# Inverse softmax sums moved from the probabilities to the weighted values in three attention layers

## The reference, cut to what matters

```python
# layer 0: 16 heads of 32; layer 1: 16 query heads of 32, 4 key heads, sparse mask; layer 2: 8 heads of 64, 1 key head
scores = jnp.einsum('bhqd,bhkd->bhqk', qn, kn) + attn_bias
p = jax.nn.softmax(scores, axis=-1)
o = jnp.einsum('bhqk,bhkd->bhqd', p, v)
o = jnp.transpose(o, (0, 2, 1, 3)).reshape(Bs, Lx, Cx)
x = x + (o @ Wproj.T + bproj) * gamma1        # layer 0 alone has gamma and a projection bias
```

## Time and profile before

| | |
|---|---|
| median of 3 runs | 2899.52 us (2898.2 to 2907.24) |
| profiled execution | 2904.38 us, span from first to last instruction 2902.6 us |
| mean granted TensorE clock | 0.894 |
| PE busy | 2427.1 us, 84% of the span |
| DVE busy | 1624.0 us, 56% |
| ACT busy | 1213.8 us, 42% |
| POOL busy | 908.3 us, 31% |

### The profile page before, as it was taken

The page is one execution under the profiler, slowest core; times in us unless marked ns, Lnnn a source line. Parts: engine busy times, 40 slices in busy tenths (PEclk is TensorE's granted clock), DMA queues, the critical chain, the costliest instruction groups (busy, mean ns, idle before and its releaser), DMA issues. The chain is left out here.

```text
span 2902.6 us, 47820 instructions
## 1 busy us (share of the span) xinstructions
PE 2427.1 (84%) x15668; PEld 1962.4 (68%) x15668; DVE 1624.0 (56%) x4635; ACT 1213.8 (42%) x2990; POOL 908.3 (31%) x982
## 2 busy tenths in 40 slices
PE   4878789798589999688888568889689999996786
PEld 2767677677477888466666457777578888885565
DVE  3777766677654443566556466566543333333876
ACT  2565565566331111366656445556431111112443
POOL 0234332233376676223223113223212112110422
PEclk7989889899899999788678679999899999997898
DMA  6000000000200000100000000000101000001000
GB/s 230 1 1 1 9 2 9 1 2 9 88 15 30 15 29 0 71 30 2 2 1 1 31 4 1 1 0 1 46 20 37 30 22 22 0 0 47 1 29 29
DMA packets 15887, 63.16 MB, mean 22 GB/s; under 512 B 2604, under 2 KB 3500, under 8 KB 10692
## 3 DMA queue, kind: packets, MB, share of 16 engines
q1 hardware_dynamic: 15684, 60.65, 5.8%
HBM read 56.42 MB, written 4.23 MB: 21 GB/s over the span
## 5 line engine op out<-in xcount | busy, mean ns | idle before, releaser
L871 ACT ACTIVATE l0a_prob<-l0a_prob,l0a_nmin 128x512 f32<-128x512 f32 x256 | 185.8, 726 | 202.9 <-DVE l0a_nmin L1129 202.5
L1673 POOL TENSOR_TENSOR l2m_hidl<-l2m_hid,l2m_hidh 128x512 fp32r<-128x512 f32 x64 | 100.9, 1577 | 480.2 <-DVE l2m_hidh L1645 480.2
L1293 POOL TENSOR_TENSOR l0a_prob<-l0a_prob,l0a_rinv 128x512 f32<-128x512 f32 x64 | 66.7, 1042 | 517.9 <-DVE l0a_rinv L1136 517.9
L1529 ACT ACTIVATE l2m_gate<-l2m_psG 128x512 f32<-128x512 f32 x64 | 38.3, 598 | 452.0 <-PE l2m_psU L1462 452.0
L1640 DVE TENSOR_TENSOR l2m_hid<-l2m_gate,l2m_psU 128x512 f32<-128x512 f32 x64 | 44.0, 688 | 300.1 <-ACT l2m_gate L1529 300.1
L702 PE MATMUL l0a_psT<-res_ident,l0a_prob 128*128 128x128 f32 x1024 | 166.2, 287 | 12.0 <-ACT l0a_PT L881 11.8
L1129 DVE CUSTOM_DVE_ANT_0 l0a_prob<-l0a_psS,l0a_mask 128x512 f32<-128x512 f32 x256 | 173.3, 688 | 2.6 <-issue 1.6
L1692 POOL TENSOR_TENSOR res_X<-res_X,l0m_share 128x512 f32<-128x512 f32 x128 | 161.8, 1292 | 25.7 <-DVE l0m_share L1629 24.7
L680 PE MATMUL l0a_psS<-l0a_kT,l0a_qT 96*128 96x512 f32 x256 | 127.9, 501 | 43.5 <-DVE l0a_nmin L1129 28.6
L560 PE MATMUL l0a_psA<-l0a_wh,l0a_hTh 128*128 128x128 f32 (+1 forms) x512 | 152.2, 297 | 12.7 <-DVE l0a_wl L1244 5.8
L702 PEld LDWEIGHTS l0a_psT<-res_ident,l0a_prob 128*128 128x128 f32 x1024 | 133.9, 148 | 38.9 <-ACT l0a_PT L881 17.9
(11 more groups left out here) (399 smaller groups left out, 7785.3 us busy)
## 6 DMA issues: line engine op xcount, KB each, us to landing
l2m_stage<-in_l2m_w SPq DMA_DIRECT2D x8, 1536.0 KB, 6.7
l0m_stage<-in_l0m_w SPq DMA_DIRECT2D x8, 1024.0 KB, 4.8
cond_w<-in_wmod SPq DMA_DIRECT2D x6, 1024.0 KB, 7.9
res_X<-in_x SPq DMA_DIRECT2D x4, 1024.0 KB, 13.4
l0a_prob<-in_l0a_w SPq DMA_DIRECT2D x4, 1024.0 KB, 6.6
l1a_wmod<-in_wmod SPq DMA_DIRECT2D x4, 1024.0 KB, 6.0
out<-res_X SPq DMA_DIRECT2D x4, 1024.0 KB, 4.3
l_stage<-in_l_w SPq DMA_DIRECT2D x3, 1024.0 KB, 7.2
```

Source lines behind the costliest of these rows:

```text
L871: act.activation(prob[:, n % NP, 0:w], src[:, 0:w], ACT.Exp, bias=nmin[:, n % NP:n % NP + 1], scale=-1.0, accum_out=ssum[:, n % NP:n % NP ...
L1293: op = pool.tensor_tensor(x, x, r.to_broadcast([P, w]), ALU.mult)
L1673: pool.tensor_tensor(hidl[:, s % 2, m, :], hid[:, m, :], f32(hidh[:, s % 2, m, :]), ALU.subtract).then_inc(hl_done, 1)
```

## The change

POOL no longer multiplies the probabilities; they are turned and weighed as exp gave them. Per unit it writes one tile `rwide`: the four inverse sums of each query, repeated over the 32 (L2: 64) features of each head, 128 x 128 (L2: 128 x 256). Twice in a group a new PE job "rT" turns two such tiles (step 9 of the group and step 2 of the next) into psA, and ACT copies them to SBUF tile rT, which then lies as psO does: features down, queries across. After the group's last `weigh`, DVE multiplies psO by rT into rT (`o_scale`, step 7). `o_copy` moves to step 8 and `o_rest` to step 9, and both read rT. The next group's `weigh` waits for `o_scale` alone. In L0 the tile bG is gone: G holds first the row to add, then gamma, with a second load between, and POOL adds to X at the end of a batch. L0's output jobs move from steps 9, 10, 11, 20 to 10, 11, 19, 21. The conditioning tiles shrink, padded copies of them are made where they are used (`padded_rows`), and the small table `pick` is loaded in three places.

```diff
+                    elif kind == "rT":
+                        pe.wait_ge(rw_done, 4 * g + 2 * x + 2)
+                        for o in range(NO):
+                            for t in range(2):
+                                c0 = (2 * o + t) * P
+                                mm = pe.transpose(psA[i][:, c0:c0 + P], rwide[:, t, o, :], R.ident[:])
+                        mm.then_inc(rT_mm, 1)
+                        freed[i] = [(rT_done, 2 * g + (x + 1))]
...
-                    pe.wait_ge(p_done, b * NTILE + (m + 1))
+                    pe.wait_ge(exp_done, b * NTILE + (m + 1))
...
-                        pe.wait_ge(oh_done, b * NG * NO + u // NT * NO)
-                        pe.wait_ge(ol_done, b * NG * NO + u // NT * NO)
+                        pe.wait_ge(on_done, b * NG * NO + u // NT * NO)
...
+                    elif kind == "rT":
+                        act.wait_ge(rT_mm, 2 * g + (x + 1))
+                        if x == 0:
+                            act.wait_ge(ol_done, NO * g)
+                        act.activation(rT[:, :, x * 2 * P:(x + 1) * 2 * P],
+                                       psA[i][:, 0:NO * 2 * P].rearrange("p (o q) -> p o q", o=NO),
+                                       ACT.Copy).then_inc(rT_done, 1)
...
+                def o_scale(b, hg):
+                    v.wait_ge(pv_done, b * U + (hg + 1) * NT)
+                    v.wait_ge(rT_done, 2 * (b * NG + hg + 1))
+                    for o in range(NO):
+                        v.tensor_tensor(rT[:, o, :], psO[o][:], rT[:, o, :], ALU.mult).then_inc(on_done, 1)
...
-                        act.activation(oTh[:, k, :], psO[o][:], ACT.Identity, bias=bias).then_inc(oh_done, 1)
+                        act.activation(oTh[:, k, :], rT[:, o, :], ACT.Identity, bias=bias).then_inc(oh_done, 1)
...
-                        for j in range(4):
-                            s = (4 * u + j) % NP
-                            x, r = prob[:, s, 0:w], rinv[:, s:s + 1]
-                            if j == 0:
-                                op = pool.tensor_tensor(x, x, r.to_broadcast([P, w]), ALU.mult)
-                            else:
-                                op = pool.tensor_scalar(x, x, r, 1.0, ALU.mult, ALU.mult)
-                            op.then_inc(p_done, 1)
...
+                def widen(b, u, first):
+
+                    pool.wait_ge(rinv_done, b * U + u + 1)
+                    if u % 2 == 0 and not (first and u == 0):
+                        pool.wait_ge(rT_mm, b * 2 * NG + u // 2)
+                    r = rinv[:, u % 2].rearrange("p (o j) -> p o j", o=NO)[:, :, :, None].to_broadcast(
+                        [P, NO, 4 // NO, HD])
+                    pool.tensor_tensor(rwide[:, u % 2].rearrange("p o (j d) -> p o j d", d=HD), r,
+                                       R.zero[:, :, None, None].to_broadcast([P, NO, 4 // NO, HD]),
+                                       ALU.add).then_inc(rw_done, 1)
...
-        OUT_AT = (9, 10, 11, 20) if is0 else (12, 13, 14, 15)
+        OUT_AT = (10, 11, 19, 21) if is0 else (12, 13, 14, 15)
+        RT_AT = {9: (0, 0), 2: (-1, 1)}
...
-                        sp.dma_start(G[:], bcast_rows(D["gam_rows"][0, b])).then_inc(g_in, 16)
-                        sp.dma_start(bG[:], bcast_rows(D["gam_rows"][1, b])).then_inc(g_in, 16)
+                        sp.dma_start(G[:], bcast_rows(D["gam_rows"][1, b])).then_inc(g_in, 16)
+                        sp.wait_ge(xg_done, b + 1)
+                        sp.dma_start(G[:], bcast_rows(D["gam_rows"][0, b])).then_inc(g_in, 16)
```

More of the change, by code:

```diff
@@ L114, in modulation_products, with modulation_sums, padded_rows @@
     return mm
-def modulation_sums(pe, R, rows, ps):
+def modulation_sums(pe, pick, rows, ps):
     for m in range(NK):
-        mm = pe.matmul(ps[:, m * B:(m + 1) * B], rows[:, m * P:(m + 1) * P], R.pick[:], start=True, stop=True)
+        mm = pe.matmul(ps[:, m * B:(m + 1) * B], rows[:, m * P:(m + 1) * P], pick[:], start=True, stop=True)
     return mm
+def padded_rows(pool, R, c32, c32_zero, c32_done):
+    pool.memset(c32[:], 0.0).then_inc(c32_zero, 1)
+    pool.wait_ge(c32_zero, 1)
+    pool.tensor_copy(c32[:, 0, :, 0:B], R.sc[:])
+    pool.tensor_copy(c32[:, 1, :, 0:B], R.cT[:]).then_inc(c32_done, 1)
 def modulation_bias(v, R, g, ps):
@@ L149, in condition @@
         rows = S.sb("rows", [P, 2, C])
+        pick = S.sb("pick", [P, B])
+        c32 = S.sb("c32", [P, 1, NK, COLS])
+        c32_zero = S.sem("c32_zero")
         pm = [S.ps(f"pm{i}", [P, 512]) for i in range(2)]
@@ L205, in sums @@
                         pe.wait_ge(mod_read, g - 1)
-                    modulation_sums(pe, R, rows[:, g % 2], ps[g % 2]).then_inc(mod_sum, 1)
+                    modulation_sums(pe, pick, rows[:, g % 2], ps[g % 2]).then_inc(mod_sum, 1)
                 pe.wait_ge(silu_done, 1)
@@ L441, in jobs @@
             todo = []
+            if s in RT_AT and n <= NTILE + 2 and not (first and n == 2):
+                todo.append(("rT", hg + RT_AT[s][0], RT_AT[s][1]))
             if hg < NG:
@@ L486, in banked @@
         def banked(first, more, last):
-            n_, out = 0, []
+            n_, out = int(first), []
             for n in range(NTILE + (OUT_AT[-1] + 2 if last else 0)):
@@ L900, in batch @@
                             pT_copy(b, m - CL, first)
[L901 removed]
+                        if n % GS == LAG + 2 and n <= NTILE + LAG + 2 and not (first and n == LAG + 2):
                             o_copy(b, n // GS - 1)
@@ L1150, in o_rest @@
                         bias = R.vb[:, k:k + 1] if is0 else R.zero[:]
-                        v.scalar_tensor_tensor(oTl[:, k, :], psO[o][:], bias, f32(oTh[:, k, :]), ALU.add,
+                        v.scalar_tensor_tensor(oTl[:, k, :], rT[:, o, :], bias, f32(oTh[:, k, :]), ALU.add,
                                                ALU.subtract).then_inc(ol_done, 1)
@@ L1219, in batch @@
                                 norm_rows(b + 1, NORM_T.index(s - NORM0 + 1))
-                        if s == LAG + 2 and n <= NTILE + LAG + 2 and not (first and n == LAG + 2):
+                        if s == LAG + 1 and n <= NTILE + LAG + 1 and not (first and n == LAG + 1):
+                            o_scale(b, hg - 1)
+                        if s == LAG + 3 and n <= NTILE + LAG + 3 and not (first and n == LAG + 3):
                             o_rest(b, hg - 1)
@@ L1305, in _ @@
-                with pool.Fori(0, B) as b:
-                    batch(b)
+                if is1:
+                    padded_rows(pool, R, c32, c32_zero, c32_done)
+                def widen(b, u, first):
[7 more added lines that the diff above has]
+                                       ALU.add).then_inc(rw_done, 1)
@@ new lines, in batch @@
+                def batch(b, first):
+                    for u in range(U):
+                        widen(b, u, first)
+                    if is0:
+                        pool.wait_ge(g_in, 32 * b + 16)
+                        for t in range(NT):
+                            x = R.X[:, b * NT + t, :]
+                            add = pool.tensor_tensor(x, x, G[:], ALU.add)
+                        add.then_inc(xg_done, 1)
+                batch(0, True)
+                with pool.Fori(1, B) as b:
+                    batch(b, False)
```

85 lines of the change are left out of this document (46 added, 39 removed).

## The result

The changed kernel takes 2941.8 us (median of 4 runs, 2938.9 to 2945.4), the kernel before 2899.7 on the same chip: ratio 1.013, 95% interval 1.0109 to 1.0151. (The ratios here are estimates from all runs, not quotients of two medians; that quotient would be 1.0145. So the loss is 38 us by the ratio and 42 by the medians.) The forecast was 2912 in a range of 2873 to 2950. The sign is right and the time lies in the range, but the loss is three times the 12 us of the forecast. The profiled execution spans 2943.5 us.

A forecast was written before the change was run, and what follows sets the result against it. PE's work, and behind it PE's waits, was taken to bound the kernel. Terms 20 + 20 + 3 - 35 + 3 - 2 + 3 = +12 us on 2904.4 gave 2916, with the runs' median 4.9 lower 2912; range 2873 to 2950.

The forecast's parts named there:

- products gone (stalls, waits): All layers: without POOL's products, DVE's stalls give back 35 us and PE's waits for POOL 2.
- places of o_copy, o_rest, output: Moved steps of these jobs: no term for the moves themselves; ACT's wait for o_rest in step 9 put at nothing.
- loads, padded condition, additions: Extra load of `pick`, twice at a layer's start: 1 us; G loaded twice at a batch's end: nothing.
- PE's turns: Four turns per 0.60 us, 33 us at the layers' clocks; 8, 6 and 6 taken as paid: +20, bounds 10 and 33.
- widen, the wait for rwide, o_rest: PE's wait for rwide in step 9, +3 us; stalls given back by `widen` and the exposed o_rest, +3.
- ends of layers: Layer tails: o_scale now stands between `weigh` and `o_copy`, 0.7 us each, 2 us for three layers.
- Nothing, while DVE leads there: Step 9: ACT's copy waits for o_rest, but ACT would wait for DVE's next minima anyway: no cost.
- signs of error: PE waiting over 6 us for rwide, DVE idle before o_scale, L0 over 15 us shorter, L1's clock far from 0.77.
- Removed stalls: DVE held up beside POOL's products, 40 us in L0, 4 in L1, 13 in L2; 60% reaches the end: -35.
- ACT and DVE: ACT's copies and DVE's o_scale in all layers: 7, 7 and 6 us, sum +20; bounds 5 and 45.
- The new wait: Job "rT" in step 9 waits for inverse sums, then `widen`; half counted: +3 us, bounds 0 and 6.
- Everything added is paid: Rival: all layers pay PE 33, others 26, wait 6, stalls -18: +51 us, 2950; chance 0.14, shared with POOL in the way.

The follow-up runs named there:

- run 1: Kernel before, each of GpSimd's products shrunk to one element, division by the sums left out: 2881.9 us, ratio 0.9918.
- 10: Kernel before with products shrunk to one element and the change's places of o_copy, o_rest and L0's output jobs: 2904.7 us, ratio 1.0014.
- run 7: From kernel 4, o_scale gone too; o_copy and o_rest read psO in the changed kernel's steps 8 and 9: 2907.9 us, ratio 1.002.
- kernel 4: From kernel 2, the "rT" jobs left out on PE and ACT, o_scale adds zero to psO: 2921.2 us, ratio 1.0058.
- kernel 2: Changed kernel with rwide written once with ones, no `widen` and no waits for it: 2939.7 us, ratio 1.0123.
- 6: From kernel 2, PE makes the turns but ACT does not copy them, o_scale adds zero: 2925.2 us, ratio 1.0083.
- Runs 7 to 10: No o_scale, 1.002; kernel 4 with o_copy, o_rest in old steps and the product behind, 0.9969; places alone, 1.0045; places without products, 1.0014.
- run 9: Kernel before with only o_copy and o_rest one step later and L0's output jobs moved: 2916.4 us, ratio 1.0045.
- run 5: Changed kernel with each turn of rwide made twice on PE: 2947.3 us, ratio 1.0145.
- 3: Changed kernel with L1's turning jobs one step later (10 and 3 for 9 and 2): 2940.8 us, ratio 1.012.

## Why the forecast was right in sign and wrong in size

By differences of ratios along the ladder of runs (each good to some 0.3%, 9 us). The rows are run 1; 10 less 1; 7 less 10; 4 less 7; 2 less 6; 6 less 4; the changed kernel less 2:

```
                                     forecast us   measured
products gone (stalls, waits)           -37        -0.82%  -24
places of o_copy, o_rest, output          0        +0.96%  +28
loads, padded condition, additions       +1        +0.06%   +2
o_scale                              (with the     +0.38%  +11
ACT's copies of rT                    next: 20)    +0.40%  +12
PE's turns                              +20        +0.25%   +7
widen, the wait for rwide, o_rest        +6        +0.07%   +2
ends of layers                           +2        within the others
sum                                     +12        +1.30%  +38
```

- **The step that failed** is that the moved o_copy and o_rest had no term at all. For o_scale the forecast asked who stands behind it and who waits, but for o_rest it asked only for ACT's copy in step 9 ("Nothing, while DVE leads there"). The order rows of the changed kernel in L0 show L1199 directly ahead of the COPY L1186, one tile nearer to it than before. None of its signs of error named PE's wait for DVE's copy. Runs 7 to 10 show the cost, 13 us alone and 28 where the stalls are gone. That takes the whole gain. How it comes about is seen in L2 (run 9); in L1 it stays open, and about half of run 9's loss there is PE's slower clock.
- **The two rows hang together.** Taken the other way round, the places first, they are +13 and -9 us. In either order they make +4 where the forecast had -37.
- **Luck.** Without the row of the places the measured rows sum to +10 us, almost the forecast's 12. But that is two errors that cancel: the removal was put at 37 us and is 24, the additions at 49 and are 34.
- **Removed stalls.** That they exist and go was right (L85, L1106, POOL's 44.7 us in L0), and so was their size: DVE's busy time fell by 40, 4 and 12 us in run 1, for estimates of 40, 4 and 13. The share that reaches the end was too high: 24 us of these 57, for 35 + 2. L1118 in L2 reached 513 ns, not 430, because seven of its 28 ran beside the wider `widen` (0.61 us) and took 719 to 802 ns. The Trainium skill (SBUF — State Buffer, "SBUF: two separate sides") says that the port pair which DVE and GpSimd share is an exclusive lock, held for a whole instruction by the one that starts first. By that rule the trace agrees: the longest L85 (383 ns) started 0.06 us after a `widen` and ended 0.05 us behind it. That o_rest with its two SBUF inputs would be held up was not put to the test: at no place do the 48 o_rest of the changed kernel run beside a POOL instruction (their median in L0 is 748 ns).
- **PE's turns.** Mis-sized: 20 for 7 (and these 7 are within the noise). Four turns by themselves take 0.60 us, but 0.11 each when they stand in a row of others (run 5), so the whole is 19 us and not 33. The rest falls into PE's idle time, 92 us in L0, 77 in L1 and 50 in L2. PE's busy time in the three layers grew by 33 us, and I first read that as turns paid in full. Doubling them added 19, and kernel 2, with them, has 18 more than kernel 4 without, so some 14 us of the growth are not the turns. I put these down to the clock, which no run shows.
- **ACT and DVE.** 23 us by runs 4, 6 and 7 against a term of 20: right, as far as the noise tells.
- **The new wait.** 9.9 us of PE's waits in L1, beyond the bound of 6, and yet its removal gained 2 or 3 us, which the noise does not tell from nothing (runs 2, 3). The forecast took the size of a wait for its price, and so did its sign of error.
- **Ends.** The 0.76 us of idle time came out as worked out (0.7 forecast). The half clock behind it, 2.5 us in L0, was not foreseen; it is not in every execution (below). In all the ends grew by 10.6 us in the profiled executions, for a forecast of 2; the ladder has this in its other rows, as no run parts the ends from the stretches.
- **G** at nothing and **pick** at 1: right, as far as the noise tells (run 7 against 10).
- **Rivals.** "Everything added is paid" came nearest in time (2950), with other terms: PE's turns were paid in small part and the wait hardly.

## What to carry to other kernels

Where engines run in lockstep over tiles, moving an instruction can cost as much as adding one (13 us for moves alone, 11 for DVE's 48 new products). List each moved instruction with what it now stands directly ahead of on its queue, and price that neighbour's waiter. A long line among the waits is no price: remove it once, and see whether the next line grows by it. And measure an added instruction by doubling it: the turns that I had at 20 us cost 4 when made a second time, and surely less than 12. Where two parts of a change act on the same wait, as products and places do here, what each is worth depends on which is taken first; give both orders.
